# Graph attention with residual norm: the last four pairs of tiles in another order

## What is computed

```python
q, k, v = heads(x @ Wq + bq), heads(x @ Wk + bk), heads(x @ Wv + bv)
scores = einsum('bhqd,bhkd->bhqk', q, k) / sqrt(32)
scores = where(adj[:, None] == 0, -inf, scores)
out = einsum('bhqk,bhkd->bhqd', softmax(scores), v)   # back to (128, 64, 512)
y = x + out @ Wo + bo
return (y - mean(y)) / sqrt(var(y) + 1e-5)             # over the 512 features
```

## Time and profile before

| what | value |
|---|---|
| median of 3 runs | 834.78 us (834.78 to 836.15) |
| the profiled execution | 834.85 us, of which 832.9 us are the span of its instructions |
| busy: PE, DVE, POOL, ACT | 816.5, 549.4, 518.2, 231.2 us |
| mean granted clock of PE | 0.995 |

### The profile page before, as it was taken

One profiled execution on the slowest core, in us unless ns is written; L12 is line 12 of the kernel. 1 busy time (PEld: TensorE's weight loads), 2 busy tenths in 40 slices (PEclk: granted clock), 3 DMA queues, 4 the chain that ended last, 5 costly groups with the idle time before them and its releaser, 6 DMA issues.

```text
span 832.9 us, 25505 instructions
## 1 busy us (share of the span) xinstructions
PE 816.5 (98%) x11276; PEld 668.3 (80%) x11276; DVE 549.4 (66%) x694; ACT 231.2 (28%) x305; POOL 518.2 (62%) x401
## 2 busy tenths in 40 slices
PE   9999999999999999999999999999999999999984
PEld 7888888888888888888888888888888888888863
DVE  5656656766657766666766567666567666667685
ACT  6532223322233222233321233222332222322110
POOL 1385657566585665767656585665856657665376
PEclk9999999999999999999999999999999999999998
DMA  9234424243342433524343242433424343322433
GB/s 328 77 78 135 115 77 142 72 146 102 87 130 83 132 94 98 140 77 128 88 154 92 81 142 67 146 102 95 124 74 139 97 127 110 83 75 85 125 87 105
DMA packets 50173, 92.37 MB, mean 111 GB/s; under 512 B 11280, under 2 KB 13328, under 8 KB 47888
## 3 DMA queue, kind: packets, MB, share of 16 engines
q1 hardware_dynamic: 47952, 87.60, 35.7%
q10 hardware_dynamic: 2112, 3.15, 1.3%
HBM read 40.37 MB, written 16.78 MB: 69 GB/s over the span
## 4 chain that ended last, share of the span: by engine, by line
PE 94%; DVE 2%; POOL 2%; issue 1%; DMA 0%; ACT 0%; ACTq 0%; POOLq 0%; DVEq 0%
PE ring L268 22%; PE ring L269 21%; PE ring L270 21%; PE ring L345 6%; PE ring L346 6%; PE ring L349 6%; PE psum_s L319 6%; PE ring L334 5%; POOL row L177 1%; POOL qt L177 0%; POOL soft L167 0%; DMA qt<-in_wq 0%; POOL rstd L732 0%; ACTq L489 0%; DVE v L574 0%
## 5 line engine op out<-in xcount | busy, mean ns | idle before, releaser
L724 POOL TENSOR_TENSOR soft<-soft,top 128x1024 f32<-128x1024 f32 x62 | 125.5, 2024 | 75.1 <-DVE top L589 75.1
L167 POOL TENSOR_TENSOR soft<-soft,inverse 128x1024 f32<-128x1024 f32 x62 | 119.0, 1921 | 25.4 <-DVE inverse L596 22.6
L470 ACT ACTIVATE kt<-ring,bk 128x512 f32<-128x512 f32 x64 | 43.6, 682 | 278.7 <-PE ring L270 278.7
L701 POOL TENSOR_TENSOR x_lo<-x_raw,x_hi 128x512 fp32r<-128x512 f32 x56 | 71.8, 1284 | 63.8 <-ACT x_hi L455 63.8
L593 DVE TENSOR_REDUCE total<-soft 128x16 f32<-128x1024 f32 x62 | 75.6, 1220 | 42.4 <-ACT soft L475 42.4
L268 PE MATMUL ring<-wv_hi,x_hi 128*128 128x512 f32 x256 | 103.2, 403 | 0.0
L268 PE MATMUL ring<-x_hi,wk_hi 128*128 128x512 f32 x256 | 103.2, 403 | 0.0
L268 PE MATMUL ring<-x_hi,wq_hi 128*128 128x512 f32 x256 | 99.8, 390 | 0.5 <-DVE x_lo L630 0.5
L269 PE MATMUL ring<-wv_lo,x_hi 128*128 128x512 f32 x256 | 100.0, 391 | 0.0
L270 PE MATMUL ring<-x_hi,wk_lo 128*128 128x512 f32 x256 | 99.9, 390 | 0.0
L269 PE MATMUL ring<-x_lo,wk_hi 128*128 128x512 f32 x256 | 99.8, 390 | 0.0
(11 more groups left out here) (74 smaller groups left out, 1370.4 us busy)
## 6 DMA issues: line engine op xcount, KB each, us to landing
pt<-soft SPq DMA_DIRECT2D x472, 64.0 KB, 2.0
x_raw<-in_xt SPq DMA_DIRECT2D x15, 1024.0 KB, 7.3
row<-in_x SPq DMA_DIRECT2D x60, 256.0 KB, 2.9
out_rows<-row SPq DMA_DIRECT2D x60, 256.0 KB, 2.4
adj<-in_adj SPq DMA_DIRECT2D x16, 128.0 KB, 2.7
pt<-soft ACTq DMA_DIRECT2D x24, 64.0 KB, 2.3
kt<-in_wk SPq DMA_DIRECT2D x4, 256.0 KB, 5.0
row<-in_wv SPq DMA_DIRECT2D x1, 1024.0 KB, 7.8
```

The costliest lines, as they stand in the source:

```text
L167: ops.tensor_tensor(soft_of(c), soft_of(c), on_keys(inverse[:, c % 2, :]), ALU.mult).then_inc(done, 1)
L701: nc.gpsimd.tensor_tensor(x_lo[:, buf, :, rows], x_raw[:, :, rows], x_hi[:, buf, :, rows].bitcast(F32), ALU.subtract).then_inc(x_lo_done, 1)
L724: nc.gpsimd.tensor_tensor(soft_of(c), soft_of(c), on_keys(top[:, c % 2, :]), ALU.subtract).then_inc(centred, 1)
```

## The change

FULL becomes 28, so that the tail holds the last four pairs, and the tail is written anew on all queues.

- Scores of pairs 29, 30 and 31 each come earlier among the projections. K and Q for the last group, V and output projections are laid between the scores; output projections come later.
- `v` and `pt` get four slots instead of two; `place(c)` waits for tile c - 4 to be mixed, and not for c - 2. The placements of tiles T-8 to T-5 are issued half by SP and half by ACT, those of T-4 and T-3 wholly by SP (before: half and half), those of T-2 and T-1 half and half as before.
- POOL gets one more tiny instruction for a row (`make_shift`: minus mean times rstd), and ACT scales and shifts rows T-10 to T-2 (`norm_by_act`). POOL normalises no row any more, DVE only row T-1.
- The adding of a row and its statistics are two functions (`add_y`, `row_sums`), so that DVE can do the second later. POOL normalises the softmax of tile T-1 instead of DVE.
- The mixed rows of the last pair are read and split tile by tile (`read_last_ot`, `split_last_ot`). `project_out(T-3)` stands behind the last mixes on PE.
- The output projections always use banks 2 and 3 of `ring`, and the mixed rows of the last pair banks 0 and 1.

The diff of what stands outside the tails, cut.

```diff
@@ -28,7 +28,12 @@
 AX_XY = mybir.AxisListType.XY
-FULL = PAIRS - GT // 2
+FULL = PAIRS - GT
+SHARED = (*range(GT), *range(TILES - 8, TILES - 4), TILES - 2, TILES - 1)
+ACT_ROWS = TILES - 10
 WARM_START = 12
...
-        v = sb("v", [P, 2, D])
+        v = sb("v", [P, 4, D])
...
-        pt = sb("pt", [P, 2, 2, HEADS, SQ])
+        pt = sb("pt", [P, 4, 2, HEADS, SQ])
...
@@ -128,15 +132,10 @@
         def ot_banks(p):
-            if p == FULL:
-                return s_banks(0, 2)
-            return ring[:, 0:2, :] if p > FULL else ring[:, 2:4, :]
+            return ring[:, 0:2, :] if p == PAIRS - 1 else ring[:, 2:4, :]
         def y_bank(c):
-            if c < 2 * FULL:
-                return ring[:, 2 + c % 2, :]
-            n = c % 2 + (2 if c < 2 * FULL + 2 else 0)
-            return s_banks(n, n + 1)[:, 0, :]
+            return ring[:, 2 + c % 2, :]
         def soft_of(c):
...
+        def mixed_rows(p, tiles):
+            chunks = slice(tiles.start * KC, tiles.stop * KC)
+            return ot_banks(p).rearrange("p g (t q) -> p t g q", q=NODES)[:, chunks]
+        def by_chunk(ot, tiles):
+            return ot[:, tiles, :, :].rearrange("p t c (g q) -> p (t c) g q", g=2)
+        def ot_count(c):
+            return c // 2 + 1 if c < TILES - 1 else PAIRS + 1
         def norm_row(eng, ops, c):
             eng.wait_ge(row_rstd, c + 1)
+            done = last_done if c == TILES - 1 else row_done
             ops.tensor_scalar(row_of(c), row_of(c), moments[:, c % 8, 0:1], rstd[:, c % 8, :],
-                              ALU.subtract, ALU.mult).then_inc(row_done, 1)
+                              ALU.subtract, ALU.mult).then_inc(done, 1)
...
             def place(c):
                 sp.wait_ge(turned, c + 1)
-                wait_for(sp, mixed, c - 1)
-                for q in range(4 if GT <= c < 2 * FULL else 2):
+                wait_for(sp, mixed, c - 3)
+                for q in range(2 if c in SHARED else 4):
                     for k in range(2):
                         to, of = block_of(c, q, k)
-                        sp.dma_start(to, of).then_inc(pt_in[c % 2], DMA)
+                        sp.dma_start(to, of).then_inc(pt_in[c % 4], DMA)
             def load_row(c):
                 if c >= TILES - 4:
...
@@ -477,16 +539,30 @@
             def read_ot(p):
                 act.wait_ge(mixed, 2 * p + 2)
                 wait_for(act, y_proj, 2 * p)
-                nc.scalar.copy(by_chunk(ot_hi), mixed_rows(p)).then_inc(ot_hi_done, 1)
+                nc.scalar.copy(by_chunk(ot_hi, slice(0, 2)), mixed_rows(p, slice(0, 2))).then_inc(ot_hi_done, 1)
+            def read_last_ot(t):
+                act.wait_ge(mixed, TILES)
+                act.wait_ge(y_proj, TILES - 3 + t)
+                act.wait_ge(ot_lo_done, PAIRS - 1 + t)
+                nc.scalar.copy(by_chunk(ot_hi, slice(t, t + 1)),
+                               mixed_rows(PAIRS - 1, slice(t, t + 1))).then_inc(ot_hi_done, 1)
+            def norm_by_act(c):
+                act.wait_ge(row_shift, c - ACT_ROWS + 1)
+                nc.scalar.activation(row_of(c), row_of(c), ACT.Identity, bias=shift[:, c % 8, :],
+                                     scale=rstd[:, c % 8, :]).then_inc(row_done, 1)
             def place(c):
                 act.wait_ge(turned, c + 1)
-                wait_for(act, mixed, c - 1)
+                wait_for(act, mixed, c - 3)
                 for q in range(2, 4):
                     for k in range(2):
                         to, of = block_of(c, q, k)
-                        act.dma_start(to, of).then_inc(pt_in[c % 2], DMA)
+                        act.dma_start(to, of).then_inc(pt_in[c % 4], DMA)
             def split_w(n, kc):
                 if n == 0:
...
-                nc.vector.tensor_tensor(by_chunk(ot_lo), mixed_rows(p), by_chunk(ot_hi).bitcast(F32),
+                nc.vector.tensor_tensor(by_chunk(ot_lo, tiles), mixed_rows(p, tiles), by_chunk(ot_hi, tiles).bitcast(F32),
                                         ALU.subtract).then_inc(ot_lo_done, 1)
-            def add_row(c):
+            def split_last_ot(t):
+                tiles = slice(t, t + 1)
+                dve.wait_ge(ot_hi_done, PAIRS + t)
+                nc.vector.tensor_tensor(by_chunk(ot_lo, tiles), mixed_rows(PAIRS - 1, tiles),
+                                        by_chunk(ot_hi, tiles).bitcast(F32), ALU.subtract).then_inc(ot_lo_done, 1)
+            def add_y(c):
                 dve.wait_ge(y_proj, c + 1)
                 dve.wait_ge(row_biased, c + 1)
                 nc.vector.tensor_tensor(row_of(c), y_bank(c), row_of(c), ALU.add).then_inc(row_added, 1)
+            def row_sums(c):
                 dve.wait_ge(row_added, c + 1)
                 nc.vector.bn_stats(stats[:, c % 8, :], row_of(c)).then_inc(row_stats, 1)
                 dve.wait_ge(row_stats, c + 1)
                 dve.sem_inc(dve_went_on, 1)
                 nc.vector.bn_aggr(moments[:, c % 8, :], stats[:, c % 8, :]).then_inc(row_moments, 1)
+            def add_row(c):
+                add_y(c)
+                row_sums(c)
             def split_w(n, kc):
                 dve.wait_ge(w_hi_done, n * KC + kc + 1)
...
                                         ALU.pow).then_inc(row_rstd, 1)
+            def make_shift(c):
+                make_rstd(c)
+                pool.wait_ge(row_rstd, c + 1)
+                nc.gpsimd.tensor_scalar(shift[:, c % 8, :], moments[:, c % 8, 0:1], rstd[:, c % 8, :], -1.0,
+                                        ALU.mult, ALU.mult).then_inc(row_shift, 1)
             nc.gpsimd.memset(eps[:, :], EPS)
             nc.gpsimd.memset(minus_half[:, :], -0.5).then_inc(const_done, 1)
...
```

## The result

The changed kernel takes 825.59 us (median of 4 runs, 824.96 to 826.82) against 834.78 us: a ratio of 0.9887 with a 95% interval of 0.9873 to 0.9901, 9.2 us or 1.1% faster. The forecast was 824.6 us, range 823.4 to 827.8. The profiled execution took 824.96 us with a span of 823.1 us.

What follows compares the result with a forecast made beforehand. PE was taken to bound the kernel, with gains only at its end: 6.4 us from PE's waits and 3.8 us from the rows' queue, 10.2 us less, gave 824.6 us, range 823.4 to 827.8.

Steps and rivals of the forecast that it cites:

- PE bounds, and only the end can give: Whole kernel: PE is busy 98% of the span, the loop has no idle PE time, only the end can gain.
- PE's work of 86.6 us: PE from pair 28's score to the end: 26 projections, scores and mixes; without waits done at 816.1 against 823.1 us.
- A new wait of 0.6 us for VectorE: Before `project_out(T-6)`: PE waits 0.4 to 0.7 us, taken as 0.6, for DVE's split of pair 29.
- The walk through DVE: DVE's steps priced from rows, without pause from 774.8 us; split of pair 29 done at about 791.5 us.
- The rows' queue, 3.8 us: End of the tail: the last add no longer waits behind POOL's row normalising, 3.8 us of the 10.2 us gain.
- Covers: Tail: placements, reads and splits arrive before PE needs them; tightest, placements of T-6 and T-5, by about 1 us.
- my third rival: Sharing issues brings nothing: T-6 and T-5 land 2.65 us later each, DVE's stretch slides 5.3 us, 829.9 us; 3%.
- The row scaling on ACT: ACT's scaling of a row in the tail: no row shows it, bounds 0.5 and 2.08 us, taken as 0.6.
- rival 1: VectorE's stretch from 774.8 to 791 us is longer than priced: 825.4 to 828 us; 14%.
- rival 2: Row loads hold up the placements on SP, so PE also waits before `project_out(T-8)`: 825.6 to 827 us; 8%.
- Rival 4, the clock: PE's granted clock falls after a wait: one fall costs 2 to 3 us, four half-clock projections 10.9 us; 2%.

Runs made afterwards that it cites:

- experiment 6: Changed kernel plus two unread maxima over 512 columns on DVE behind the mask of tile T-2: 826.72 us, ratio 0.9904 to the kernel before.
- experiment 7: Changed kernel plus two unread maxima over 512 columns on DVE ahead of the mask of tile T-6: 825.58 us, ratio 0.9900 to the kernel before.
- experiment 1: Kernel before with only ACT scaling rows T-6 to T-2 (POOL makes the shifts): 830.91 us against 834.51, ratio 0.9961.
- experiment 4: Changed kernel with rows T-6 to T-3 normalised by POOL and T-2 by DVE again: 826.49 us, ratio 0.9899 to the kernel before.
- experiment 3: Changed kernel with placements of T-8 to T-5 issued by SP alone: 832.79 us, ratio 0.9973 to the kernel before.
- experiment 5: Changed kernel with the last pair's mixed rows read by one copy and one split: 825.94 us, ratio 0.9899 to the kernel before.
- experiment 2: Changed kernel with placements waiting as with two slots, `v` keeping four: 841.55 us, ratio 1.0079 to the kernel before.

## Why the prediction was right, step by step

- *PE bounds, and only the end can give.* Right. From the start of the tail to the last add the kernel before takes 827.15 - 729.54 = 97.6 us, the changed one 817.33 - 730.01 = 87.3 us. Of the 10.3 us between them, PE's end, counted from the same start, gives (823.1 - 729.54) - (817.1 - 730.01) = 6.5 us (forecast 6.4) and the gap between PE's end and the last add 4.0 - 0.2 = 3.8 us (forecast 3.8). The 0.47 us by which the new tail starts later arose in the loop, whose order the change leaves alone (only the waits for buffers differ); it is within what the traces scatter (729.1 to 730.7).
- *PE's work of 86.6 us.* Mis-sized by half a microsecond: with no wait at all PE took 817.1 - 730.0 = 87.1. With 26 projections at 2.72 us, scores, mixes and what they cost the matmul behind them take 87.1 - 70.7 = 16.4 us, where I had 15.9: the error is in their price, 3.57 us for a pair's scores and mixes from the loop, and in the 1.6 for the extra mixes.
- *A new wait of 0.6 us for VectorE.* This step failed in its size: the wait was zero. The walk through DVE was right to 0.3 us, counted from the start of the tail (split done at 791.73 - 730.01 = 61.7 us after it, forecast 791.5 - 729.54 = 62.0), but PE, with its longer work, came 0.2 us later still. The two errors cancel, which is luck; the sum, 87.4 us from tail to last add, met 87.3. That VectorE is within a hair of being the pace in that stretch, and not before the mask of T-6, is shown by experiments 6 and 7.
- *The rows' queue, 3.8 us.* Right as a single step from the old order (experiment 1, 3.6 us) and as the gap that closes at the end. But it is not what ACT's scaling is worth in the new order: without it that order loses only 0.9 to 1.2 us (experiment 4), since the rows are then added early enough for POOL to do two of them in time.
- *Covers.* Sharing of the issues held `mask(T-4)` in time, its loss costs 7.2 us (experiment 3), more than the 5.3 of my third rival, since that had no clock in it. Reading by tiles hides a wait of 1.24 us (experiment 5). The row scaling on ACT, with no row before, cost 0.8 us and not 0.6, within its bounds and hidden.
- *Rivals 1 and 2.* The median, 825.59, lies just above my own band of 823.6 to 825.4, in the range that rival 1 names (from 825.4) and at the edge of rival 2's (825.6). But neither happened: in the trace PE has no wait for DVE, and the masks of pair 30 none for landed blocks.
- *Rival 4, the clock.* It didn't happen here; it did in experiment 1, as in the kernel before, in 2 and 3, and in the loop of 7. Behind waits of 7.76 and 4.25 us and a pause of 2.01 us the granted clock had means of 0.50, 0.67 and 0.58 over 4 us; with waits of 1.2 us among dense projections (experiments 5 and 6) it stayed at 1.00 to the end of PE. A projection at the lower level, 0.50, cost 5.41 us and not 2.81 (experiment 2). This agrees with the Trainium skill (TensorE: Matmul & The Clock Gate, What's actually happening), which lets the clock follow how busy the array has been.
- The median lies 1.0 us above the forecast, the profiled execution, the fastest of the four, 0.4 us. The rest may be scatter from run to run, for which experiment 7 shows one source; whether it is the one in the timed runs, no trace tells.

Not tried: the deeper buffers alone, in the old order; the softmax of tile T-1 back on DVE (2.08 us of its work in the old order).

## What to carry to other kernels

When one engine is busy for 98% of the span, cost the tail as a schedule: walk the two or three engines through it with start-to-start times from the rows. The single steps came out within half a microsecond here; that the sum came out closer still was luck. An order that brings work forward is worth only as much as the buffers let through, so look first at the waits that protect a buffer: here the same order with two-slot waits is 16 us slower than with four. And don't price a long stall by its length alone: behind the waits of 4.25 and 7.76 us PE lost another 1.7 and 2.6 us at a lower clock.

## What was not expected of the hardware

- Eight placements issued by SP took 4.94 us at 774.96, and 5.64 us shortly before, with no placement on ACT. Side by side, eight on SP and eight on ACT took 5.98 us each at 795.00 and 5.36 and 5.05 us at 763.68 in the changed kernel, and 4.96 and 5.29 us at 808.75 in the kernel before. So the price of eight issues varies between 4.9 and 6.0 us, and the rows don't show that the two queues slow each other.
- A single stall of PE's queue of 2.01 us in the loop, with no releaser, cost the whole pipeline 3.9 us in that pair, the fall of the clock included. The same three matmuls at the end of the same mix waited 0.60 us in experiment 6 (at 542.49), 0.15 us in experiment 2 (at 542.14), and not at all in the other traces. The cause stays open.
- Scaling a row of 512 columns on ACT with scale and bias from memory took 0.82 us, where `read_k`, with a bias alone and from the accumulator memory, takes 0.68 us in the page. Two things differ, and no run separates them.

The row of SP with nothing on ACT:

```profile
768.60 5.64 SPq L201 DMA_DIRECT2D pt<-soft  x8
```

The pause in experiment 6:

```profile
542.49 0.30 PE L351 MATMUL ring<-pt,v 64*32 64x64 f32 x3 [0.60 <-issue]
```
